# A mixture-of-experts kernel: the second weights of each expert as two f16 halves, three f16 products in place of one f32 product

## What is computed

```python
logits = (x @ gate_w + gate_b) / TEMP            # 8 experts, the best 2 are kept
h = gelu(einsum('bsd,edf->bsef', x, w1) + b1)    # w1: 8 x 512 x 2048, f32
expert_out = einsum('bsef,efd->bsed', h, w2) + b2  # w2: 8 x 2048 x 512, f32
out = einsum('bse,bsed->bsd', gate_probs, expert_out)
x = x + layernorm(out) * ln_g + ln_b
```

## Time and profile before

| | |
|---|---|
| median of 3 runs | 1471.23 us |
| the profiled execution | 1469.05 us, its span 1467.4 us |
| PE busy | 1382.4 us (94%), 8042 instructions |
| DVE busy | 781.0 us (53%) |
| ACT busy | 586.5 us (40%) |
| POOL busy | 156.8 us (11%) |
| DMA | 207.52 MB, mean 141 GB/s |

### The profile page before, as it was taken

One profiled execution on the slowest core, in us unless ns is written; L12 is line 12 of the kernel. 1 busy time (PEld: TensorE's weight loads), 2 busy tenths in 40 slices (PEclk: granted clock), 3 DMA queues, 4 the chain that ended last, 5 costly groups with the idle time before them and its releaser, 6 DMA issues.

```text
span 1467.4 us, 24647 instructions
## 1 busy us (share of the span) xinstructions
PE 1382.4 (94%) x8042; PEld 879.9 (60%) x8043; DVE 781.0 (53%) x1871; ACT 586.5 (40%) x1082; POOL 156.8 (11%) x200
## 2 busy tenths in 40 slices
PE   6879999999999999999996899999999999999997
PEld 5658677686676876768764544444444444444442
DVE  5665876868777777787665532222222222232225
ACT  3565665756747567466670211212112121121100
POOL 1001012020020200302003100000000000000005
PEclk9999999999999999999999999999999999999997
DMA  9793142341322412325028807524325166100005
GB/s 363 269 351 144 52 154 92 116 161 50 134 102 104 182 50 109 127 79 209 29 91 329 320 28 279 217 83 158 135 105 196 44 256 249 44 21 21 14 15 172
DMA packets 53568, 207.52 MB, mean 141 GB/s; under 512 B 4902, under 2 KB 5012, under 8 KB 47388
## 3 DMA queue, kind: packets, MB, share of 16 engines
q1 hardware_dynamic: 40320, 123.14, 22.7%
q0 software_dynamic: 13184, 83.89, 14.9%
q10 hardware_dynamic: 28, 0.01, 0.0%
HBM read 144.11 MB, written 62.91 MB: 141 GB/s over the span
## 4 chain that ended last, share of the span: by engine, by line
PE 80%; DVE 8%; ACT 4%; issue 4%; POOL 2%; DMA 1%; SPq 0%; DVEq 0%; ACTq 0%; POOLq 0%
PE bank L624 22%; PE bank L1466 8%; PE bank L1424 7%; PE bank L606 6%; PE bank L608 5%; PE bank L607 5%; PE bank L1387 4%; PE bank L1492 4%; PE bank L1408 3%; PE bank L616 3%; PE bank L1433 2%; PE bank L1448 2%; PE bank L1514 2%; ACT moe_w L954 2%; DVE moe_w L1115 2%
## 5 line engine op out<-in xcount | busy, mean ns | idle before, releaser
L624 PE MATMUL bank<-moe_w,arena 128*128 x736 | 330.9, 592 | 0.0
L492 DVE SCALAR_TENSOR_TENSOR arena<-bank,now_scales,arena 128x512 f32<-128x512 f32 x92 | 69.1, 751 | 344.0 <-PE bank L608 344.0
L624 PEld LDWEIGHTS bank<-moe_w,arena 128*128 128x128 f32 x736 | 132.7, 190 | 132.5 <-issue 132.5
L1424 PE MATMUL bank<-moe_w 128*128 128x257 f32 x768 | 189.8, 385 | 6.5 <-DVE moe_w L886 6.5
L429 ACT ACTIVATE arena<-arena 128x512 f32<-128x512 f32 x92 | 58.3, 633 | 335.7 <-DVE arena L492 335.7
L1424 PEld LDWEIGHTS bank<-moe_w 128*128 128x128 f32 x768 | 138.2, 192 | 25.6 <-DVE moe_w L886 5.8
L606 PE MATMUL bank<-moe_w,arena 128*128 x368 | 139.7, 379 | 1.3 <-POOL pool_mark L384 1.3
L607 PE MATMUL bank<-moe_w,arena 128*128 x368 | 139.5, 379 | 0.0
L608 PE MATMUL bank<-moe_w,arena 128*128 x368 | 139.5, 379 | 0.0
L1466 PE MATMUL bank<-moe_w 128*128 128x512 f16 x384 | 114.4, 379 | 10.0 <-ACT moe_w L943 7.0
L929 ACT ACTIVATE moe_w<-bank,cols,ugain 128x512 f32<-128x512 f32 x96 | 74.6, 777 | 61.6 <-PE bank L1467 60.8
(11 more groups left out here) (234 smaller groups left out, 2158.4 us busy)
## 6 DMA issues: line engine op xcount, KB each, us to landing
moe_w<-w_halves POOLq DMA_DIRECT2D x8, 4096.0 KB, 13.2
moe_w<-in_L_ffn_w_dram POOLq DMA_DIRECT2D x8, 4096.0 KB, 24.4
w_halves<-moe_w SPq DMA_DIRECT2D x48, 512.0 KB, 3.1
xs_rows<-blocks SPq DMA_DIRECT2D x8, 2048.0 KB, 14.8
moe_w<-in_L_ffn_w_dram SPq DMA_DIRECT2D x16, 1024.0 KB, 6.3
arena<-in_ctx_dram SPq DMA_DIRECT2D x32, 384.0 KB
arena<-in_L_ffn_w_dram SPq DMA_DIRECT2D x8, 1024.0 KB, 4.8
blocks<-in_L_ffn_w_dram SPq DMA_DIRECT2D x8, 1024.0 KB, 4.8
```

What stands on the lines that cost most here:

```text
L492: nc.vector.scalar_tensor_tensor(out=h_sb[:, fb % 2, :], in0=bank[fb % 2][:, :], scalar=now_scales[:, KD:KD + 1], in1=b1_rows[:, bass.ds(s ...
L624: last = nc.tensor.matmul(Y[:, :], hT_sb[:, fb % 2, c, :], moe_flat[:, bass.ds((e % 2) * 16384 + 8192 + (4 * fb + c) * DIM, DIM)], start=( ...
L1424: last = nc.tensor.matmul(bank[h][:, 0:KEYS], qkT[:, c, b, h * P:(h + 1) * P], cnT[:, b % 2, c, :], start=(c == 0), stop=(c == KC - 1))
```

## The change

The second weights are no longer read as f32 by `mm2`. In every job, for each block, ACT rounds 128x2048 of `w2` to f16 with one scale for each expert (`v_hi`, two instructions of 1024 columns) and DVE makes the low half (`v_lo`, two of 1024). The transposed block is split likewise (`h_hi` on ACT, `h_lo` on DVE in place of `hT_copy`). `mm2` then issues three f16 matmuls for each of its four slices, and `y_copy` multiplies the scale back. The halves have two buffers each, by block parity, in tiles that the first stage has done with (`y`, `yT`, `kqT`, `v_sb`, `wosT`, parts of `arena` and `blocks`). DVE keeps the scales of the current job in four small tiles and copies each anew once a job, and it reads the next job's expert number (`scales_now(j + 1)`) after the last block of the job before.

To get the scales, the first stage now loads all of `w2` once (`raw2_load`, 1 MB pieces, four for each group) and sums its absolute values on ACT (`row_sums2`): two pieces at a group's end, two inside the next group; the last group does all four. `b1` is loaded and summed once. Loads go into areas that a group uses otherwise (`raw2`), so the copies at the top of the next group wait for the sums, and the next group's first piece of `w1` is loaded later.

The 16 diagonals move behind the last `y_copy`, because `y`, `yT`, `kqT` and `v_sb` now hold halves of weights; `x_all + ln_b` is split, four adds after job 0 and four after job 1.

```diff
@@ moe_act
+            def h_hi(j, fb):
+                act.wait_ge(hT_full, FB * j + fb + 1)
+                if fb >= 2 or not isinstance(j, int) or j > 0:
+                    act.wait_ge(mm2_done, 1 + FB * j + fb - 1)
+                nc.scalar.activation(hT_high[:, fb % 2, :, :].rearrange("p c t -> p (c t)"), bank[2 + fb % 2][:, :], ACT.Identity,
+                                     scale=now_h[:, 0:1]).then_inc(hT_high_done, 1)
+            def v_hi(j, fb, slot):
+                if fb >= 2 or not isinstance(j, int) or j > 0:
+                    act.wait_ge(mm2_done, 1 + FB * j + fb - 1)
+                for i in range(2):
+                    nc.scalar.activation(v_high[fb % 2][i], moe_flat[:, bass.ds(slot * 16384 + 8192 + fb * 2048 + i * 1024, 1024)],
+                                         ACT.Identity, scale=now_v[:, 0:1]).then_inc(v_high_done, 1)
+            def job(j, first, last):
...
+                gelu(j, 0)
+                if not first:
+                    h_hi(j - 1, 3)
+                act.wait_ge(now_h_ok, j + 1)
+                v_hi(j, 0, slot)
+                gelu(j, 1)
+                h_hi(j, 0)
+                v_hi(j, 1, slot)
+                gelu(j, 2)
+                h_hi(j, 1)
+                v_hi(j, 2, slot)
+                if not last:
+                    x_hi(j + 1)
+                gelu(j, 3)
+                h_hi(j, 2)
+                v_hi(j, 3, slot)
@@ moe_dve
+            def h_scales_now(j, e):
+                if not isinstance(j, int) or j > 0:
+                    dve.wait_ge(hT_out, FB * j)
+                    dve.wait_ge(v_low_done, 2 * FB * j)
+                nc.vector.tensor_copy(now_v[:, :], job_scales[:, bass.ds(e, 1), KD + 1])
+                nc.vector.tensor_copy(now_h[:, :], job_scales[:, bass.ds(e, 1), KD + 2]).then_inc(now_h_ok, 1)
...
+            def v_lo(j, fb, slot):
+                for i in range(2):
+                    dve.wait_ge(v_high_done, 2 * (FB * j + fb) + i + 1)
+                    nc.vector.scalar_tensor_tensor(out=v_low[fb % 2][i], in0=moe_flat[:, bass.ds(slot * 16384 + 8192 + fb * 2048 + i * 1024, 1024)],
+                                                   scalar=now_v[:, 0:1], in1=v_high[fb % 2][i],
+                                                   op0=ALU.mult, op1=ALU.subtract).then_inc(v_low_done, 1)
...
             def job(j, first, last=False):
...
+                b_scale_now(j, e)
                 bias(j, 0, slot)
                 if not first:
-                    hT_copy(j - 1, 3)
+                    h_lo(j - 1, 3)
+                    v_lo(j - 1, 3, slot_of(j - 1))
+                h_scales_now(j, e)
+                if not last:
+                    dve.wait_ge(xt_out, j + 1)
+                    scales_now(j + 1)
                 bias(j, 1, slot)
-                hT_copy(j, 0)
+                h_lo(j, 0)
+                v_lo(j, 0, slot)
                 if not first:
                     y_copy(j - 1)
+                y_scale_now(j, e)
                 bias(j, 2, slot)
...
@@ moe_pe, mm2
+                pe.wait_ge(v_low_done, 2 * (FB * j + fb + 1))
                 for c in range(4):
-                    last = nc.tensor.matmul(Y[:, :], hT_sb[:, fb % 2, c, :],
-                                            moe_flat[:, bass.ds((e % 2) * 16384 + 8192 + (4 * fb + c) * DIM, DIM)],
-                                            start=(fb == 0 and c == 0), stop=(fb == 3 and c == 3))
+                    high, low = [part[fb % 2][c // 2][:, (c % 2) * DIM:(c % 2 + 1) * DIM] for part in (v_high, v_low)]
+                    nc.tensor.matmul(Y[:, :], hT_low[:, fb % 2, c, :], high, start=(fb == 0 and c == 0), stop=False)
+                    nc.tensor.matmul(Y[:, :], hT_high[:, fb % 2, c, :], high, start=False, stop=False)
+                    last = nc.tensor.matmul(Y[:, :], hT_high[:, fb % 2, c, :], low, start=False, stop=(fb == 3 and c == 3))
@@ first stage, the loads of a group
+                if later:
+                    sp.wait_ge(sum2_done, KD * (g - 1) + 3)
+                    raw2_load(g - 1, 3, raw2)
+                    sp.wait_ge(sum2_done, KD * g)
+                    raw_load(g, 0)
...
+                sp.wait_ge(m_full, M_FILLS * g + O_AT + 2)
+                raw2_load(g, 0, raw2)
+                raw2_load(g, 1, raw2)
...
@@ first stage, ACT (and the same two waits on DVE)
+                if do_b and do_a:
+                    act.wait_ge(sum2_done, KD * (g - 1) + 2)
+                    act.wait_ge(b1_summed, 1)
                 for i in range(QK_PAIRS):
                     if do_a:
                         qk_copy(act, nc.scalar.copy, g, i, 1)
+                    if i == 3 and do_b and do_a:
+                        row_sums2(g - 1, 2, raw2)
```

More of the change, by code:

```diff
@@ L429, in gelu @@
                 nc.scalar.activation(h_sb[:, fb % 2, :], h_sb[:, fb % 2, :], ACT.Gelu).then_inc(h_act, 1)
-            x_hi(0)
[L432 to L438, removed]
+            def h_hi(j, fb):
[11 more added lines that the diff above has]
+            def job(j, first, last):
+                slot = act.value_load(job_e[0:1, bass.ds(j, 1)], min_val=0, max_val=EXPERTS - 1) % 2
+                gelu(j, 0)
[14 more added lines that the diff above has]
+                v_hi(j, 3, slot)
+            x_hi(0)
+            job(0, True, False)
+            with act.Fori(1, JOBS - 1) as j:
+                job(j, False, False)
+            job(JOBS - 1, False, True)
+            h_hi(JOBS - 1, 3)
         def moe_dve(dve):
@@ L544, in moe_dve, with x_and_beta @@
             x_lo(0)
+            def x_and_beta(first, n):
+                for t in range(first, first + n):
+                    last = nc.vector.tensor_tensor(x_all[:, t, :], x_all[:, t, :], lnrow[:, 1, :], ALU.add)
+                return last
             job(0, True)
             dve.wait_ge(rows_in, 48)
-            for t in range(GROUPS):
-                last = nc.vector.tensor_tensor(x_all[:, t, :], x_all[:, t, :], lnrow[:, 1, :], ALU.add)
-            last.then_inc(xb_done, 1)
+            x_and_beta(0, GROUPS // 2)
             job(1, False)
+            x_and_beta(GROUPS // 2, GROUPS // 2).then_inc(xb_done, 1)
+            with dve.Fori(2, JOBS - 1) as j:
+                job(j, False)
+            job(JOBS - 1, False, True)
+            h_lo(JOBS - 1, 3)
+            v_lo(JOBS - 1, 3, slot_of(JOBS - 1))
+            y_copy(JOBS - 1)
             for t in range(GROUPS):
@@ L656, in moe_pe @@
                 job(j, False, False)
-            e = job(JOBS - 1, False, True)
+            job(JOBS - 1, False, True)
             hT_fill(JOBS - 1, 3)
-            mm2(JOBS - 1, 2, e)
-            mm2(JOBS - 1, 3, e)
+            mm2(JOBS - 1, 2)
+            mm2(JOBS - 1, 3)
             pe.wait_ge(rows_in, 48)
@@ L955, in row_sums, with row_sums2 @@
                                      accum_out=row_sum[:, k:k + 1]).then_inc(sum_done, 1)
+            def row_sums2(g, k, of):
+                act.wait_ge(raw2_in[k], 16 * (g + 1))
+                if k == (0 if of is raw2 else 2):
+                    at_least(act, sums2_kept, g)
+                nc.scalar.activation(of[k].bitcast(F16)[:, 0:FF], of[k], ACT.Abs, bias=tiny[:, 0:1], scale=W_SUM,
+                                     accum_out=row_sum2[:, k:k + 1]).then_inc(sum2_done, 1)
             def w_hi(g, k):
@@ L1022, in body @@
                     w_hi(g, 3)
+                    if not nxt:
+                        row_sums2(g, 2, raw2_last)
+                        row_sums2(g, 3, raw2_last)
+                    row_sums2(g, 0, raw2)
+                    row_sums2(g, 1, raw2)
+                    if isinstance(g, int) and g == 0:
+                        act.wait_ge(b1_in, 16)
+                        nc.scalar.activation(b1_raw, b1_raw, ACT.Abs, bias=tiny[0:EXPERTS, 0:1], scale=W_SUM,
+                                             accum_out=b1_sum[:, :]).then_inc(b1_summed, 1)
             act.wait_ge(consts, 7)
@@ L1615, in body @@
                     pe.wait_ge(most_step, 1)
[L1616 removed]
+                    nc.tensor.transpose(M[1][0:2 * EXPERTS, 0:P], most[:, :], ident[:, :]).then_inc(most_full, 1)
                 if do_b:
```

155 lines of the change are left out of this document (107 added, 48 removed).

## The result

The changed kernel takes 1486.39 us, median of 4 runs (1486.13 to 1488.17); the kernel before took 1470.66 in the same session. The ratio is 1.011, 95% interval 1.0094 to 1.0126. I had forecast 1437 us, range 1412 to 1461: wrong, on the other side of no change.

A forecast was written before the change was run, and what follows sets the result against it. PE was taken as the bound; 22 jobs at 24.2 instead of 26.35 us gave -47.3, once-only terms +0.3, +4.2, +4.7, +0.9 and +3.0, sum -34.2: 1437 us. Own range 1424 to 1450, 8-in-10 range 1412 to 1461.

The forecast's parts named there:

- PE alone 22.95 us: Repeated job if only PE's own time counted, with f16 `mm2`: 22.95 us instead of 26.35.
- The circle 24.2 us: One job's chain of waits through DVE, ACT and PE: 24.1 us, plus 0.1 for address registers, 24.2 a job.
- my dear end: Costly bounds on the circle's steps: `v_lo` pairs 2.48, `v_hi` 2.2, `h_hi` at the gelu's 0.63; job then 24.8 us.
- my rival: Circle longer through register reads behind waits and PE to ACT hand-overs: 25.2 us a job, 1459 us; chance 16%.
- PE stands still 1.25 us in each, where it never stood before: PE's pause in every job before block 0's `mm2`, ended by the copy of `Y`: 1.25 us.
- the row: Profile times of the `v_lo` operation, 2.343 us on 2048 columns and 0.553 on 384, giving 1.24 at 1024.
- First stage and scales +3.9: Once-only cost before the experts: first stage's loads and sums +3.0 us, five small DVE scale operations +0.9.
- Job 0 with the additions +4.5: Once-only: job 0's first `mm2` waits, +0.3 us; `x_all + ln_b` adds after jobs 0 and 1, +4.2.
- The diagonals +3.2: After the last copy of `Y`: 16 diagonals on DVE, for which PE's bias products wait, +3.2 us.
- PE stays the bound: Rival: scale copies or `Y`'s copy come off the circle; job 22.95 us, kernel 1409.5 us; chance 14%.
- Expert loads starve: Rival: DVE operations hold up POOL, which issues expert loads; at loads of 60 us, 1506 us; chance 4%.
- Sums late at the group boundary: Rival: first-stage loads and sums end 6 us late in all eight groups; 1485 us; chance 4%.

The follow-up runs named there:

- runs 8 and 9: run 8, then the same with the eight `ln_b` additions spread over jobs 2 to 9, one behind each bias of block 2: 1397.70 us, ratio 0.951.
- run 1: Changed kernel with 16 idle products on PE in each job's pause, ahead of block 0's `mm2`: 1461.25 us, ratio 0.994 to the kernel before.
- run 4: Changed kernel with the copy of `Y` moved on DVE ahead of `h_lo` of block 0: 1442.43 us, ratio 0.981 to the kernel before.
- run 8: Changed kernel with scales in two sets, register read at the job's head, two banks for `Y` and the diagonals ahead of its last copy: 1401.67 us.
- Run 10: Changed kernel without the 32 loads and sums of the second weights in the first stage, scales from a constant: 1485.19 us, ratio 1.011.
- run 2: Kernel before with six idle DVE additions ahead of `Y`'s copy in the repeated jobs, so PE pauses, unfilled: 1567.65 us, ratio 1.067.
- run 7: Changed kernel with only `now_v` and `now_h` in two sets, written at the job's head, loops over pairs of jobs: 1424.42 us, ratio 0.968.

## Why the prediction was wrong

- **PE alone 22.95 us**: right (22.90 in runs 8 and 9; the f16 pitch is 0.2155).
- **The circle 24.2 us**: right in its path and in what ends PE's pause, 1.1 us too short. Its steps were mis-sized by 0.22 (PE to `h_lo`), 0.39 (`h_lo`, `v_lo` of block 3), 0.21 (to ACT), 0.13 (`v_hi`, gelu, `h_hi`) and 0.27 (`h_lo`, `v_lo`, `Y`), of which I had put in 0.1. `h_hi` took 0.677, over the gelu's 0.63 that was my dear end; `v_lo` 1.28 and `v_hi` 1.14. The register read in front of `v_lo` stood in my rival and not in my sum. This rival, 25.2 us a job and 1459 us, was right to 0.1 us a job, and run 1, the changed kernel at full clock, takes 1461.25. 21 x 1.1 is 23 us of the error.
- **The step that failed** is "PE stands still 1.25 us in each, where it never stood before". The pause is 2.12 us, and I priced it at its own length: I took for granted that the products behind it run at the same speed, a term put at nothing without a reason. They did not: 15 distances between copies are 1.7 us longer by a stretch at 1.2 GHz, 25 us, and run 1 gets back 25.1. With the circle's 23 this is 48 of the 51 us.
- **The two are not independent.** In run 4 the pause is 1.27 us, about what I had forecast; no half clock followed it in the repeated jobs, and the kernel took 1442.43 us against my 1437. So, as far as this one run shows, the price was right for the pause that I forecast, and the circle's 1.1 us carried the pause to a length at which the clock falls.
- **What before showed.** In its jobs PE never paused. Behind the last job it did, 1.37 us ahead of the 16 bias products, and there the granted clock was 0.60, in the changed kernel 0.50 (columns as in run 1; before first):

```profile
1428.84:1440.51 11.67, 11.67 (x17) 4.27 (x17) 0.00 (x0) 0.00 (x0) 7.70 (x8) 0.60 0.54 152
```

```profile
1444.09:1458.11 14.02, 14.02 (x17) 5.22 (x17) 0.00 (x0) 0.00 (x0) 8.38 (x9) 0.50 0.64 187
```

I read these products' 11.67 us and did not look at their clock. The Trainium skill, page "TensorE: Matmul & The Clock Gate", section "HAM oscillation — how this bites in real kernels", describes such a drop once in every turn of a loop in which TensorE waits. The trace agrees in part: a drop follows 15 of the 19 pauses of 2.1 us between 915 and 1397 us, not every one. The prediction did not weigh it.

- **`v_lo`.** The formula of the Trainium skill's page "VectorE: DVE Perf Modes", section on the TRN2 errata, gave an estimate of 1.22 us at 1024 columns. Measured: 1.28, so the row was the better guide and still low.
- **Once-only terms.** First stage and scales +3.9, measured +2.7. Job 0 with the additions +4.5, measured 8.0: +5.6 to the first copy, and 2.4 by which the next distance is over 25.3. Of the 5.6, about 4 is the copy's new place: it starts 4.4 us after the products of its job end, behind `v_lo`, and before it started after 0.2. The diagonals +3.2, measured 2.95 (PE waits 4.32 us for them and the copies, before 1.37). The bias products behind them took 14.02 us instead of 11.67, which no term had. That the once-only terms come near their sum is in part luck.
- **Rivals.** "PE stays the bound" named the true cure, scales and `Y` off the circle, and run 8 gives its 22.9. "Expert loads starve" is out: expert 2's comes in 27.4 us (887.35 to 914.80) against 27.8. "Sums late at the group boundary" is out by the +2.7.

The table loads of gelu left the loop, as forecast. What stays open is why the clock stayed full after four of the 19 pauses (those that end at 942.4, 1102.8, 1236.1 and 1396.5 us). Run 10, which only starts 3.6 us earlier, has another pattern of long and short distances. This suggests that it matters where the pause falls in time; no run fixes it more closely.

## What to carry to other kernels

An engine that has been the bound without a gap may lose more from its first gap than the gap: before you trade TensorE's work for a wait, look for the granted clock behind any gap of its kind, and fill the gap with idle products as a quick test. When work moves to engines that were idle, what counts is not their sum (18 of 23 us here) but the longest circle of waits through them, and every tile with one copy (`now_v`, `Y`) closes such a circle: a second copy of three small tiles, with a register read moved, gave 2.1 us a job, and a second bank for `Y` the last 0.3. By then PE itself is the limit, at 22.9 us. A hand-over's price is all that has to wait behind it, not its own 0.6 us.

## What I had not expected of the hardware

- Half clock follows 15 of 19 pauses of 2.1 us (changed kernel) and nearly all of 2.9 us (run 2) in a PE that is otherwise busy all the time, and none of the 20 of about 1.27 us in run 4. Where between them the change lies, no run shows.
- PE's idle products cost nothing measurable to DVE or ACT: in run 1 the circle stays at 25.3 us.
- Behind a wait of DVE for its own last result stands a register read, and 0.71 us of "issue" that goes with the wait (run 7). The read in front of `v_lo`, which has no such wait ahead, shows 0.26 in both kernels. That the read is what the time is spent on is my reading of the order, not shown by itself.
